# Weight products copied by ScalarE, first tiles summed on landing, chosen rows handled once per two groups, and engine lists in a new order

## The reference, cut to what matters

```
pooled = x.reshape(64, 12, 14, 16, 14, 16).sum(axis=(3, 5))
h  = einsum('bcij,ce->bije', pooled, channel_weights)      # 64 x 196 x 192
a  = layernorm(h)                                          # = y in the attention
   attention, 12 heads of 16, causal; only k_sel = 14 tokens per image are kept,
   the top_k of softmax((a @ sel_w + sel_b) / temperature)[..., 1]
   y = a with (attn(a) @ out_w + out_b) * selection added at these 14 rows
h  = h + y
out = h + gelu(layernorm(h) @ in_weight.T + in_bias) @ out_weight      # 192 -> 768 -> 192
```

## Time and profile before

| | us |
|---|---|
| median of 3 runs | 705.06 |
| profiled execution | 706.07 |
| its span | 704.4 |
| TensorE matmul busy | 576.7 (82%) |
| VectorE busy | 522.0 (74%) |
| ScalarE busy | 335.0 (48%) |
| GpSimd busy | 251.9 (36%) |
| granted TensorE clock, mean | 0.942 of full |

### The profile page before, as it was taken

One profiled execution on the slowest core, in us unless ns is written; L12 is line 12 of the kernel. 1 busy time (PEld: TensorE's weight loads), 2 busy tenths in 40 slices (PEclk: granted clock), 3 DMA queues, 4 the chain that ended last, 5 costly groups with the idle time before them and its releaser, 6 DMA issues.

```text
span 704.4 us, 12381 instructions
## 1 busy us (share of the span) xinstructions
PE 576.7 (82%) x3860; PEld 475.4 (67%) x3860; DVE 522.0 (74%) x1103; ACT 335.0 (48%) x826; POOL 251.9 (36%) x484
## 2 busy tenths in 40 slices
...
GB/s 326 348 363 193 302 350 174 342 276 343 240 336 268 300 253 345 285 302 222 331 302 275 209 232 320 247 309 246 333 302 289 227 331 140 13 10 41 26 9 40
...
## 3 DMA queue, kind: packets, MB, share of 16 engines
...
## 4 chain that ended last, share of the span: by engine, by line
PE 44%; DVE 18%; issue 16%; POOL 8%; DMA 6%; ACT 5%; POOLq 1%; DVEq 0%; SPq 0%; ACTq 0%
PE psO L637 15%; DMA X<-in_x 6%; PE psS L588 6%; DVE R L942 5%; PE psS L597 4%; PE psF L625 4%; PE psS L576 3%; PE psA L542 2%; DVE mx L1056 2%; PE psS L561 2%; ACT ET L754 2%; POOL b_ln L391 1%; DVE a_ln L952 1%; DVE b_ln L954 1%; DVE y_ln L956 1%
## 5 line engine op out<-in xcount | busy, mean ns | idle before, releaser
L942 DVE TENSOR_REDUCE R<-X 128x42 f32<-128x2688 f32 (+1 forms) x112 | 260.5, 2339 | 15.6 <-POOL X L352 8.5
L637 PE MATMUL psO<-W,act 128*112 128x192 f32 x1344 | 261.8, 339 | 11.9 <-ACT obuf L779 4.0
L637 PEld LDWEIGHTS psO<-W,act 128*112 128x112 f32 x1344 | 223.3, 183 | 18.2 <-issue 7.3
L772 ACT ACTIVATE act<-psF 128x392 f32<-128x392 f32 x192 | 95.3, 496 | 123.1 <-PE psF L625 121.2
L352 POOL TENSOR_TENSOR X<-X 128x1344 f32<-128x1344 f32 x32 | 96.9, 3027 | 21.3 <-DMA X<-in_x 21.1
L361 POOL TENSOR_TENSOR Pt<-Praw 48x196 f32<-48x196 f32 x16 | 8.6, 538 | 191.3 <-DMA Praw<-patch_sums 191.3
L625 PE MATMUL psF<-Stk,M1S 104*128 104x392 bf16 x192 | 66.1, 344 | 5.5 <-ACT act L772 4.8
L1067 DVE TENSOR_TENSOR G<-psS,K 64x336 f32<-64x336 f32 x32 | 16.0, 501 | 44.7 <-PE psS L588 44.2
L588 PE MATMUL psS<-ET,F 98*64 98x336 f32 x128 | 39.6, 452 | 10.4 <-ACT ET L754 10.4
L750 ACT ACTIVATE Sm<-Sm,rinv 112x196 f32<-112x196 f32 x96 | 35.3, 445 | 18.9 <-DVE rinv L1062 18.7
L745 ACT ACTIVATE Sm<-psS,nm 112x196 f32<-112x196 f32 x96 | 39.2, 427 | 7.3 <-DVE nm L1059 7.2
...
(10 more groups left out here) (197 smaller groups left out, 954.1 us busy)
## 6 DMA issues: line engine op xcount, KB each, us to landing
...
patch_sums<-R ACTq DMA_DIRECT2D x16, 147.0 KB, 7.9
Praw<-patch_sums ACTq DMA_DIRECT2D x16, 147.0 KB, 6.5
...
```

What stands on the lines that cost most here:

```text
L637: pe.matmul(to, act_sb[u % 2][:, m, i * OT:(i + 1) * OT], W2[:, m, :], start=(m == 0), stop=False)
L772: act.activation(act_sb[u % 2][:, n // 2, (n % 2) * (GT // 2):(n % 2 + 1) * (GT // 2)], psF[:, 0:GT // 2], ACT.Gelu).then_inc(act_F1.sem, 1)
L942: dve.tensor_reduce(R[:, r, t * TQ * N:(t + 1) * TQ * N].rearrange("p (q j) -> p q j", q=TQ), v, AX.XY, ALU.add).then_inc(dve_L, 1)
```

## The change

Eight things are changed together.

1. The copies of the weight products from PSUM move from VectorE to ScalarE (`weights_heads`, `weights_attention` of ScalarE).
2. VectorE sums all seven tiles of group 0 before it splits the FFN's weights (`first_group`), and the tiles no longer stand between the steps of the preparation.
3. The weight loads get gates: W1T waits for tile 1 of x, the attention weights for tile 3, and W2 for tile 6; W2 gets a semaphore of its own.
4. TensorE makes group 0's moments (`tm`) ahead of its first period.
5. The output product `at` and the row `h1` are made once per two groups: G2, ZY, dsm, dsel and res have room for both, with the odd group from row 64 on.
6. The own embedding `rs` is made once per two groups, in psC, and `sc` waits for its copy no longer.
7. The chosen rows' store `c:s` moves on GpSimd from ahead of the halving of tile 5 to between d1 and d2.
8. The lists of TensorE, ScalarE and VectorE are drawn anew.

```diff
 # GpSimd
-plan = ("X:3:1 P:s:2 c:s:5 H:5:1 A:var2:2 K:v:2 K:d1:2 K:d2:2 H:0:0").split()
+plan = ("X:3:1 P:s:2 H:5:1 A:var2:2 K:v:2 K:d1:2 c:s:5 K:d2:2 H:0:0").split()
 # TensorE
-plan = ("S:et:2 o:3.0:2 o:3.1:2 o:3.2:2 S:g:2 K:tr1:1 o:4.0:2 o:4.1:2 K:tr2:1 f:0:1 o:4.2:2 A:sl:1 "
-        "at:0:2 at:1:2 f:1:1 o:5.0:2 f:2:1 at:2:2 f:3:1 A:st:1 o:5.1:2 f:4:1 G:ga:1 f:5:1 o:5.2:2 f:6:1 "
-        "G:u:1 f:7:1 o:6.0:2 o:6.1:2 f:8:1 C:xt:2 o:6.2:2 C:fa:2 f:9:1 S:sc:1 f:10:1 C:fb:2 A:tm:0 "
-        "f:11:1 C:f2:2 o:0.0:1 o:0.1:1 o:0.2:1 o:1.0:1 A:zt:0 o:1.1:1 o:1.2:1 o:2.0:1 o:2.1:1 o:2.2:1").split()
+plan = ("K:tr2:1 o:4.0:2 f:0:1 at:0:2 A:sl:1 at:1:2 at:2:2 o:4.1:2 f:1:1 o:4.2:2 f:2:1 o:5.0:2 A:st:1 "
+        "f:3:1 o:5.1:2 G:ga:1 f:4:1 o:5.2:2 f:5:1 G:u:1 f:6:1 o:6.0:2 f:7:1 C:xt:2 f:8:1 C:fa:2 S:sc:1 "
+        "f:9:1 o:6.1:2 A:tm:0 f:10:1 o:6.2:2 f:11:1 C:fb:2 o:0.0:1 o:0.1:1 o:0.2:1 o:1.0:1 o:1.1:1 "
+        "o:1.2:1 C:f2:2 o:2.0:1 o:2.1:1 o:2.2:1 S:et:1 o:3.0:1 A:zt:0 C:rs:1 o:3.1:1 S:g:1 K:tr1:0 "
+        "o:3.2:1").split()
 # ScalarE
-plan = ("S:e0:2 S:e1:2 S:e2:2 S:e3:2 S:e4:2 S:e5:2 O:0:2 S:n:2 O:1:2 A:fm:1 K:H:1 S:t:2 K:M:1 O:2:2 "
-        "K:L:1 A:e:1 O:3:2 R:st:0 K:k1:1 K:k2:1 f:0:1 f:1:1 f:2:1 f:3:1 O:4:2 R:ld:0 f:4:1 f:5:1 f:6:1 "
-        "O:5:2 f:7:1 G:rs:1 C:XH:2 f:8:1 C:ga:2 f:9:1 f:10:1 O:6:2 C:gb:2 f:11:1").split()
+plan = ("S:e5:2 O:0:2 S:n:2 O:1:2 K:H:1 S:t:2 K:M:1 A:fm:1 O:2:2 K:L:1 A:e:1 K:k1:1 R:st:0 G:rs:2 K:k2:1 "
+        "f:0:1 O:3:2 f:1:1 f:2:1 f:3:1 R:ld:0 O:4:2 f:4:1 f:5:1 f:6:1 O:5:2 f:7:1 C:XH:2 f:8:1 f:9:1 "
+        "C:ga:2 f:10:1 O:6:2 f:11:1 C:gb:2 S:e0:1 S:e1:1 S:e2:1 S:e3:1 S:e4:1").split()
 # VectorE
-plan = ("C:os:4 S:g:3 A:sel:2 L:0:0 A:top:2 S:at:3 A:slots:2 G:ga:2 C:xh:3 L:1:0 G:u:2 L:2:0 S:sc:2 "
-        "A:var:1 L:3:0 S:ri:2 L:4:0 A:log:1 L:5:0 L:6:0").split()
+plan = ("C:os:4 C:xh:3 L:0:0 G:u:2 L:1:0 S:sc:2 A:var:1 L:2:0 A:log:1 S:ri:2 L:3:0 L:4:0 L:5:0 L:6:0 "
+        "A:sel:1 S:g:2 A:top:1 S:at:2 A:slots:1 G:ga:1").split()
...
 # VectorE, ahead of its periods
+def first_group():
+    sum_tile(0, 0, 0)
+    weights_first()
+    sum_tile(0, 0, 1)
+    weights_moments()
+    sum_tile(0, 0, 2)
+    weights_tokens()
+    for t in range(3, XT):
+        sum_tile(0, 0, t)
+    weights_parts("M")
+    sum_tile(1, 1, 0)
+    weights_parts("R")
+    sum_tile(1, 1, 1)
+    stage_A(0, 0, "var")
+    stage_A(0, 0, "log")
+    weights_bias()
...
 # ScalarE, ahead of its periods
+act.wait_ge(x_in[1], loaded(0))
 act.dma_start(W1T[0:DH, :, :], w1t.rearrange("(k d) n -> d k n", k=2)).then_inc(w_ffn, 16)
 act.dma_start(W1T[DH:DH + 1, 0, :], b1).then_inc(w_ffn, 16)
+act.wait_ge(x_in[3], loaded(0))
 act.dma_start(Wqkv[0:DH, :, :], wqkv.rearrange("(k d) n -> d k n", k=2)).then_inc(w_att, 16)
...
+def weights_heads():
+    act.wait_ge(pe_W.sem, pe_W.at(0, "m1"))
+    for k in range(2):
+        ins = act.activation(M1f[:, k * HID // 2:(k + 1) * HID // 2], (psF, psC)[k][0:SK, 0:HID // 2], ACT.Copy)
+    ins.then_inc(act_W.sem, 1)
+    act.wait_ge(x_in[6], loaded(0))
+    act.dma_start(W2[:, :, :], w2.rearrange("(h p) e -> p h e", h=HT)).then_inc(w_out, 16)
...
 weights()
+weights_heads()
+step_R(0, 0, "st")
+step_R(0, 0, "ld")
+weights_attention()
 periods(nc.scalar, body, 6, 2)
...
 # TensorE, the chosen rows' own embedding and output product
+def step_rs(g, q):
+    pe.wait_ge(dve_G.sem, dve_G.at(g, "zy"))
+    if exists(g - 2):
+        pe.wait_ge(dve_C.sem, dve_C.at(q - 1, "os1"))
+    pe.matmul(psC[0:PROWS, 0:D], ZY[:, :, :].rearrange("p e s -> p (e s)")[:, 0:PROWS], BW[:, :],
+              start=True, stop=True).then_inc(pe_Q.sem, 1)
...
 def step_at(g, j):
     if j == 0:
         pe.wait_ge(dve_S.sem, dve_S.at(g, "g1"))
-    mm = pe.matmul(psS[0:SLOTS, 0, 0:D], G2[:, j, :], B2[:, j, :], start=(j == 0), stop=(j == HP - 1))
+    mm = pe.matmul(psS[0:PROWS, 0, 0:D], G2[:, j, :, :].rearrange("p e s -> p (e s)")[:, 0:PROWS], B2[:, j, :],
+                   start=(j == 0), stop=(j == HP - 1))
```

More of the change, by code:

```diff
@@ L631, in step_F2 @@
                 if m == 0:
+                    if i == 0 and isinstance(g, int) and g == 0:
+                        pe.wait_ge(w_out, 16)
+                        pe.wait_ge(dve_W.sem, dve_W.at(0, "alR"))
                     if i == 0:
```

209 lines of the change are left out of this document (108 added, 101 removed).

## The result

The changed kernel is slower. Its median is 736.25 us (732.01 to 745.91), that of the kernel before in the same session 706.68 us (704.78 to 709.79); the ratio is 1.042, with a 95% interval of 1.036 to 1.047. The forecast was 693 us and faster. The profiled execution took 736.75 us, at a mean granted TensorE clock of 0.899 instead of 0.942.

What follows compares the result with a forecast made beforehand. TensorE was taken to bound odd rounds, a wait chain through the held negative and F to the next g even ones. 706.07 - 13 (head) + 4 (pairs) - 3 (tail) = 694 profiled, 693 median; range 673 to 706.

Steps and rivals of the forecast that it cites:

- The pair's 73.7: Even plus odd round before the change; forecast to become 74.3, so +4 us over six pairs from group 0 to 12.
- What lies in even rounds was covered by a wait there, so it brings nothing: TensorE: of 23 us of matmuls removed, those in even rounds gain 0; the last round goes from 31.3 to 29.
- the load leave at 11.8: Even rounds: the sums' load leaves 11.8 us after g instead of 10.1, so P is ready at 20.9 at most.
- the store's and masks' gain: Even rounds: chosen rows' store moved and queries' masks earlier, so the negative is held less; 36.1 us, 0.9 less than 37.0.
- 38.2: Odd round in us, against 36.7: store ahead of d2 delays the halving, `sel` waits, masked product and `sl` come later.
- R3: Rival: `at` ahead of `sl` makes odd rounds 40.5, even ones stay 37, pair 77.5; 712 us, slower; chance 0.09.
- R1: Rival: lists work better, `sel` slips ahead of the halving, pair 71.5 to 73; 675 to 685 us; chance 0.25.
- Forecast 116: Head: first g at 116 us instead of 129.37, a gain of 13 us through earlier sums, store, P and F.
- The rest of the head keeps its steps: Head, after F: the steps stay as before, with VectorE's five tiles in the same stretch.
- R2: Rival: W2 ahead of the store on its queue, store lands 5 us late, head gains 8; 698 us; chance 0.13.
- The forecast's -3: Tail: last three rounds gain 0.5 + 2.3 us, the last row's FFN +-1.

Runs made afterwards that it cites:

- the last one: Changed kernel with sums' read later, sl first, chosen rows' store behind tile 0's halving, output product reissued, no loops, head store before copies, W2 behind read: 676.9 us, ratio 0.961.
- the later read: Changed kernel with the read of the sums two Gelu steps later in ScalarE's list: 709.7 us, ratio 1.006 against 1.042.
- the filler: Changed kernel with the output product issued again in even rounds, its result overwritten: 720.5 us, ratio 1.023 against 1.042.
- no loops: Changed kernel with the periods of TensorE, ScalarE and VectorE all written out: 720.0 us, ratio 1.022 against 1.042.

## Why the prediction was wrong, point by point

The profiled execution took 43 us more than the 694 of the sum: 15 in the head, 21 in the six pairs of rounds, 10 in the last three rounds, less 3 behind the last `g`. (The pair's 73.7 before the change is that of typical rounds; the six took 74.35 in the mean, as round 0 has 33.6 and round 7 has 43.3.)

**The step that failed** is the one on edits 5 and 6: "What lies in even rounds was covered by a wait there, so it brings nothing". It brings a loss. The 12 matmuls that filled a wait of TensorE kept its clock up; where they went, the clock fell behind the wait, and 2.4 us of covered work became 4 us of path. This is shown: with nothing but those matmuls put back the ratio goes from 1.026 to 0.990 with the old lists, and from 1.042 to 1.023 with the new ones (there in part by round 11, which is not theirs). The sum took each duration at the clock at which the earlier trace rows showed it. That the even round stood at 0.95 and the tail at 0.89 was there to be read the earlier trace rows. In the changed kernel the fall needs the next point too: with either undone, rounds 2, 4, 10 and 12 take 34.3 to 35.9 us instead of 37.1 to 38.5.

**Even rounds, the read.** The prediction had the load leave at 11.8. In even rounds it left at 12.0 to 13.3 (16.4 in round 8), as the store took 9.5 us in the median to land and not 7.9, and ScalarE stood at it for up to 2.9 us with Gelu steps behind. That wait was in the sum as P's delay only; what stood behind it on ScalarE was not. It is worth 25 us (1.042 to 1.006), a good half of it in the even rounds, and in these largely through the clock. The other half of this term was too small the other way: 0.9 us was forecast as the store's and masks' gain, but with the store alone moved the even rounds from 2 on fell by 2.7 us in the mean. In the changed kernel the negative is hardly held either (mean 193 ns, 1190 before), but there it starts 24.2 us after `g` or later in the even rounds from 2 to 12, when the halving is over.

**Odd rounds.** For rounds 3, 5 and 7 right in mechanism and nearly in size. `den` held 2.28 us, masked product 6.0 to 7.0 us after `g` (6.7 forecast for its end), `sl` behind it at 7.8, rounds 38.5 to 38.8 against 38.2. Two errors partly cancel in that: F came at 28.7 to 29.0 (29.3 forecast), and the next `g` 9.8 to 10.0 behind it, not 9.0. The cause was the store's new place rather than `at`: the store alone gave 38.0 to 38.3 in the kernel before, and `sl` ahead of `at` brought 0.6 us at most. R3 had the right sign for the wrong place: pairs of 75.9 to 77.3 came about in rounds 2 to 7, but through the even rounds and the clock.

**Rounds 8, 9, 11 and 13.** Not in the prediction at all, and 27 us over what they took before in the profiled executions. Two causes are shown in 8, 9 and 11: gaps of 5.1 and 3.1 us at a loop's edge, which the new lists put in mid-round (the kernel before has 5.9 us of this kind on ScalarE, in round 7); and xh against the halving of tile 5. In round 13 (40.8) the trace shows a wait of 1.5 us for xh and a low clock behind it. Round 11 took 37.7 to 38.3 us in the five other versions that keep the new lists and the store's place: its 8 us hang on when xh and the halving start, 18.3 and 18.8 us after `g` here, 17.4 to 17.6 and 19.3 to 19.7 in those five. R1's "the collision is a matter of 0.5 us" looked at `sel` and not at the entries that moved to the front of VectorE's list.

**Head.** Forecast 116, measured 131.1. Five terms failed. Tile 3 was summed at 40.95 and not at 37 (41.45 before), so the sums ended at 49.7 and not at 46. ScalarE was free at 57.4 and not at 48 to 53: the last weights landed at 47 instead of 36 to 42, gates on tiles 1 and 3 having held their issue back to 18.4. Store to P took 15.1 and not 9.2: the store landed in 9.2 us instead of 6.2, with the DMA engines at a share of 1.06 where it had been 0.71, and P came 6.0 us behind the read instead of 3.0, at a share of 0.57; why the read took so long is open. And "The rest of the head keeps its steps" was wrong: from F to `ga` it is 24.7 us, was 19.9, for VectorE's 5.1 us at B and its five tiles in one piece. The wait for B is edit 4's: the weight products went behind the moments, which the prediction priced at nothing. It is in every version with the new head, the last one too. R2 (W2 ahead of the store) was real only where the store leaves early, at 4 us, near its 5; W2 itself took 21.7 us, near the 24 of its far end. The Trainium skill's statement on queues that it rested on ("DMA: Bandwidth & Descriptors", section "Queues, rings and completion order") agrees with the landings of 14.7 and 10.8 us.

**Tail.** The forecast's -3 was for the last three rounds (0.5 + 2.3); they took 6.7 us more, rounds 12 and 13 at granted clocks of 0.91 and 0.92, and the last one fell from 31.2 to 30.7 and not to 29. What fell by 2.8 is the stretch behind the last `g`, for which the forecast had +-1: that the sizes agree is luck. It is 26.7 us in the changed kernel with the old lists and 24.2 with the new ones, so the lists gave it. TensorE work -23 us: 112 matmul instructions fewer (3748 for 3860), as said, at no gain in busy time.

How much of the 31 us is due to each edit can't be added up: the later read gives 25 us, the filler 13, no loops 14 (by the ratios), all in part the same microseconds of low clock, and in each profiled execution with the same 8 us of round 11.
